# A decoder layer with 64 experts on one core: the expert rows found from a list of places, the second tile of an expert woven into the next expert's step

## The reference

```python
router_logits = x2d @ gate_w                      # 800 rows, 64 experts
routing_weights = jax.nn.softmax(router_logits, axis=-1)
routing_weights, selected_experts = jax.lax.top_k(routing_weights, TOP_K)   # 8 of 64
routing_weights = routing_weights / jnp.sum(routing_weights, axis=-1, keepdims=True)
...
layer_w0 = jax.lax.ragged_dot(sorted_inputs, gate_k, group_sizes, preferred_element_type=jnp.bfloat16)
layer_w1 = jax.lax.ragged_dot(sorted_inputs, up_k, group_sizes, preferred_element_type=jnp.bfloat16)
intermediate = jax.nn.silu(layer_w0) * layer_w1
expert_out = jax.lax.ragged_dot(intermediate, down_k, group_sizes, preferred_element_type=jnp.bfloat16)
...
out = jnp.einsum('tke,tk->te', unsorted, routing_weights.astype(jnp.float32))
```

## Time and profile before

| | |
|---|---|
| time, median of 3 runs | 2540.93 us (2531.51 to 2547.09) |
| span of the profiled execution | 2527.7 us |
| what lies around the span, against the median | 13.2 us |
| mean granted clock of TensorE | 0.897 of full speed |
| PE busy | 2011.5 us (80%) |
| DVE, ACT, POOL busy | 45%, 26%, 19% |
| DMA | 518.81 MB, mean 205 GB/s |

### The profile page before, as it was taken

One profiled execution on the slowest core, in us unless ns is written; L12 is line 12 of the kernel. 1 busy time (PEld: TensorE's weight loads), 2 busy tenths in 40 slices (PEclk: granted clock), 3 DMA queues, 4 the chain that ended last, 5 costly groups with the idle time before them and its releaser, 6 DMA issues. The chain is left out here.

```text
span 2527.7 us, 48690 instructions
## 1 busy us (share of the span) xinstructions
PE 2011.5 (80%) x17744; PEld 1692.7 (67%) x17745; DVE 1130.7 (45%) x2122; ACT 646.6 (26%) x1391; POOL 468.2 (19%) x556
## 2 busy tenths in 40 slices
PE   5999886059298989999959899959857788877756
PEld 4999864037298978888758777736656666666622
DVE  4444510034233354444433566643365555554366
ACT  4333300033221234434321344431101111111112
POOL 0111101101000011111100111101133334332156
PEclk9999988569699989999979999979979999999965
DMA  7999997669987255555276587833459989898445
GB/s 183 214 215 222 218 239 253 235 187 228 268 215 159 78 121 137 121 129 129 66 190 162 150 198 184 191 108 81 163 181 366 353 314 416 335 373 343 176 147 161
DMA packets 148152, 518.81 MB, mean 205 GB/s; under 512 B 27154, under 2 KB 68114, under 8 KB 140858
## 3 DMA queue, kind: packets, MB, share of 16 engines
q0 software_dynamic: 31776, 215.85, 38.2%
q1 hardware_dynamic: 105162, 281.04, 30.7%
q10 hardware_dynamic: 11088, 20.19, 2.1%
HBM read 582.94 MB, written 236.06 MB: 324 GB/s over the span
## 5 line engine op out<-in xcount | busy, mean ns | idle before, releaser
L81 PE MATMUL img_acc<-img_ctx_hi,img_w_hi 128*128 128x258 f32 x1024 | 303.4, 296 | 51.4 <-DVE img_ctx_lo L1158 40.1
L82 PE MATMUL img_acc<-img_ctx_lo,img_w_hi 128*128 128x258 f32 x1024 | 295.0, 288 | 0.1
L83 PE MATMUL img_acc<-img_ctx_hi,img_w_lo 128*128 128x258 f32 x1024 | 294.7, 288 | 0.0
L1780 POOL DMA_DIRECT2D experts_bf_dram<-in_moe_dram x192 | 98.3, 512 | 871.7 <-DMA experts_bf_dram<-in_moe_dram 542.2
L81 PEld LDWEIGHTS img_acc<-img_ctx_hi,img_w_hi 128*128 128x128 f32 x1024 | 199.8, 195 | 76.1 <-issue 65.4
L1951 POOL DMA_INDIRECT moe_rows<-expert_rows_dram,moe_index x77 | 150.3, 1952 | 387.1 <-DVE moe_index L2101 382.6
L82 PEld LDWEIGHTS img_acc<-img_ctx_lo,img_w_hi 128*128 128x128 f32 x1024 | 199.9, 195 | 0.4 <-issue 0.4
L83 PEld LDWEIGHTS img_acc<-img_ctx_hi,img_w_lo 128*128 128x128 f32 x1024 | 200.0, 195 | 0.0
L81 PE MATMUL txt_acc<-txt_ctx_hi,txt_w_hi 128*128 128x320 f32 x512 | 169.5, 331 | 37.5 <-DVE txt_ctx_lo L1158 29.2
L82 PE MATMUL txt_acc<-txt_ctx_lo,txt_w_hi 128*128 128x320 f32 x512 | 161.8, 316 | 0.0
L83 PE MATMUL txt_acc<-txt_ctx_hi,txt_w_lo 128*128 128x320 f32 x512 | 161.7, 316 | 0.0
(11 more groups left out here) (321 smaller groups left out, 4332.9 us busy)
## 6 DMA issues: line engine op xcount, KB each, us to landing
experts_bf_dram<-in_moe_dram POOLq DMA_DIRECT2D x192, 768.0 KB, 8.5
routing_w<-experts_bf_dram SPq DMA_DIRECT2D x48, 2304.0 KB
moe_w_last<-experts_bf_dram SPq DMA_DIRECT2D x16, 2304.0 KB
expert_results_dram<-self_zeros POOLq DMA_DIRECT2D x19, 1536.0 KB
self_w_raw<-in_w_self_dram SPq DMA_DIRECT2D x32, 512.0 KB, 12.0
expert_results_dram<-moe_out ACTq DMA_DIRECT2D x64, 256.0 KB, 7.3
img_raw<-in_ctx_img_dram SPq DMA_DIRECT2D x8, 1032.0 KB, 6.3
cross_k_dram<-img_kT SPq DMA_DIRECT2D x64, 129.0 KB, 2.0
```

The lines of the kernel that those rows point to most:

```text
L81: eng.matmul(out, w_hi, a_hi, start=first, stop=False)
L82: eng.matmul(out, w_hi, a_lo, start=False, stop=False)
L83: return eng.matmul(out, w_lo, a_hi, start=False, stop=last)
L1780: pool.dma_start(self.dst_d[n], self.src_d[n]).then_inc(self.done[u], 16)
```

## The change

- **Results.** Each expert has a fixed area of 7 tiles (`PLACES`), so a row's place in the results is known as soon as its rank in the expert is. Nothing is blanked, and `first_tile` goes.
- **Routing.** Choice, rank and place are found batch by batch in `route_phase`. POOL writes each row's number to its place in a list in DRAM: 8 scatters of 100 numbers a batch, in turn into four lists (`scatter`), each behind the last one of its list. At the end SP loads the four lists, DVE takes the least of them (an empty place holds 800), PE turns it, and the row numbers of all experts stand in SBUF (`r.token`).
- **Experts.** The comparison and the 32 matmuls of a step go; DVE copies two columns of `r.token` (`note_token`) for expert e+2, and POOL gathers e+2 in step e, where it was e+3. PE's step now is gate of e, narrow of e-1, up of e; if e-1 has a second tile, its transposes, products and narrow stand between these, with a PSUM tile of their own for the transposes. SP waits for `expert_done`, which DVE signals at the end of the step. Code for both cases stands in each step. The routing weights are made at the start, from the 8 chosen logits.
- **Combine** takes its places from `r.places`.

```diff
-            blank = clear_d.rearrange("(c n p) d -> c p n d", p=P, c=CLEARS)
-            pool.wait_ge(cleared, 3)
-            for c in range(CLEARS):
-                wait(pool, blanked, 16 * c)
-                pool.dma_start(blank[c], zeros[:, :].unsqueeze(1).broadcast_to(blank[c].shape)
-                               ).then_inc(blanked, 16)
-            pool.wait_ge(blanked, 16 * CLEARS)
...
-                wait(sp, at_split, b - 1)
+                wait(sp, outp_ready, 2 * (b - 1))
...
+            sp.wait_ge(router_ready, B)
+            for n in range(LISTS):
+                sp.wait_ge(listed[n], 16 * B * TOP_K // LISTS)
+                sp.dma_start(list_rows[:, n], list_d[n].rearrange("(e t p) n -> e t (p n)", e=EXPERTS, p=P)
+                             ).then_inc(list_loaded, 16)
+            sp.wait_ge(list_loaded, 16 * LISTS)
...
+                pool.dma_start(list_d[n].rearrange("(p n) one -> p (n one)", p=P), empty[:, :]
+                               ).then_inc(list_cleared, 16)
+            pool.dma_start(xn_d[B * S:B * S + 1, :], no_row[:, :]).then_inc(list_cleared, 16)
...
+            def scatter(b):
+                pool.wait_ge(places_ready, b + 1)
+                for k in range(TOP_K):
+                    wait(pool, listed[k % LISTS], 16 * (b * TOP_K // LISTS + k // LISTS))
+                    pool.sem_inc(scatter_step, 1)
+                    pool.indirect_dma_start(
+                        out=list_d[k % LISTS][:, :],
+                        out_offset=bass.IndirectOffsetOnAxis(ap=r.places[:, b, k:k + 1], axis=0),
+                        in_=numbers[:, b:b + 1], in_offset=None).then_inc(listed[k % LISTS], 16)
...
+            pool.wait_ge(list_cleared, 16 * LISTS + 16)
+            for b in range(B):
+                send(b, b % 2)
+                if b + 2 < B:
+                    add_bias(b + 2, b % 2)
+                if b > 0:
+                    scatter(b - 1)
+            scatter(B - 1)
...
+            def choose(b, u):
+                dve.wait_ge(logits_ready, b + 1)
+                link(dve.max(r.top[:, b, :], logits[:, u, :]))
+                dve.max_index(which[:, :], r.top[:, b, :], logits[:, u, :])
+                link(dve.match_replace(rest[:, :], r.top[:, b, :], logits[:, u, :], SELECTED))
+                dve.tensor_tensor(chosen[:, u, :], rest[:, :], logits[:, u, :],
+                                  ALU.not_equal).then_inc(chosen_ready, 1)
+                shape = [S, TOP_K, EXPERTS]
+                link(dve.tensor_tensor(match[:, :, :], expert_no[:, :].unsqueeze(1).broadcast_to(shape),
+                                       which[:, :].unsqueeze(2).broadcast_to(shape), ALU.is_equal))
+            def find_places(b, u):
+                shape = [S, TOP_K, EXPERTS]
+                dve.wait_ge(ranked, b + 1)
+                link(dve.tensor_tensor(place[:, :], rank_ps[0:S, 0:EXPERTS], place_start[:, :], ALU.add))
+                link(dve.tensor_tensor(so_far[:, :], so_far[:, :], chosen[:, u, :], ALU.add))
+                link(dve.tensor_tensor(match[:, :, :], match[:, :, :],
+                                       place[:, :].unsqueeze(1).broadcast_to(shape), ALU.mult))
+                link(dve.tensor_reduce(place_of[:, :], match[:, :, :], AX.X, ALU.add))
+                dve.tensor_copy(r.places[:, b, :], place_of[:, :]).then_inc(places_ready, 1)
...
+            find_places(B - 2, 0)
+            choose(B - 1, 1)
+            find_places(B - 1, 1)
+            dve.sem_inc(chosen_ready, 1)
+            dve.wait_ge(ranked, B + 1)
+            tabulate()
+            dve.wait_ge(list_loaded, 16 * LISTS)
+            link(dve.tensor_tensor(least[:, :, :], list_rows[:, 0], list_rows[:, 1], ALU.min))
+            link(dve.tensor_tensor(least[:, :, :], least[:, :, :], list_rows[:, 2], ALU.min))
+            dve.tensor_tensor(list_f[:, :, :], least[:, :, :], list_rows[:, 3], ALU.min).then_inc(list_ready, 1)
+            dve.wait_ge(list_turned, 1)
+            dve.tensor_copy(r.token[:, :, :].rearrange("p t e -> p (t e)"),
+                            list_ps[:, 0:MAX_TILES_OF * EXPERTS])
...
+            def rank(b, u):
+                wait(pe, places_ready, b)
+                pe.wait_ge(chosen_ready, b + 1)
+                pe.matmul(rank_ps[0:S, 0:EXPERTS], ones[:, :], so_far[:, :], start=True, stop=False)
+                pe.matmul(rank_ps[0:S, 0:EXPERTS], before[:, :], chosen[:, u, :],
+                          start=False, stop=True).then_inc(ranked, 1)
...
+    LAG = 1
+    AHEAD = 2
...
-                    wait(sp, out_ready, e - W_SLOTS + 1)
+                    wait(sp, expert_done, e - W_SLOTS + 1)
...
+                gather(g, c + AHEAD)
...
+            def note_token(e, c):
                 if has_expert(e):
-                    wait(dve, numbered, e - 1)
-                    compare(seated[:, c % 2], e, 2 * P).then_inc(seated_ready, 1)
-            def note_rows(e, c):
-                if has_expert(e):
                     wait(dve, turned, e - W_SLOTS + 1)
-                    dve.wait_ge(numbered, e + 1)
-                    dve.tensor_copy(index[:, c % W_SLOTS, :], number_ps[:, 0:2]).then_inc(index_ready, 1)
+                    wait(dve, expert_done, e - W_SLOTS + 1)
+                    dve.tensor_copy(token[:, c % W_SLOTS, :],
+                                    r.token[:, 0:2, bass.ts(e, 1)].rearrange("p t e -> p (t e)")
+                                    ).then_inc(token_ready, 1)
...
+                    tiles = tiles_of(dve, e - 1)
+                    with dve.If(tiles > 1):
+                        x = tiles_before(dve, e - 1)
+                        x_turn_rows(x)
+                        copy_right()
+                        x_multiply(x)
+                        multiply(e, c)
+                        x_copy_right(x, x_copied)
+                        behind_second(dve, e - 1, tiles, x, tile)
+                        dve.sem_inc(expert_done, 1)
+                    with dve.Else():
+                        copy_right()
+                        multiply(e, c)
+                        dve.sem_inc(x_copied, 1)
+                        dve.sem_inc(expert_done, 1)
+                else:
+                    multiply(e, c)
...
+                turn_rows(g, c + 1)
+                if has_expert(e - 1):
+                    tiles = tiles_of(pe, e - 1)
+                    with pe.If(tiles > 1):
+                        x = tiles_before(pe, e - 1)
+                        x_turn_rows()
+                        gate()
+                        narrow_first()
+                        x_products(x)
+                        up()
+                        pe.wait_ge(x_inner_ready, x + 1)
+                        pe.wait_ge(left_copied, e)
+                        pe.wait_ge(right_copied, e)
+                        narrow(slot, x_inner, x_out_ready)
+                        behind_second(pe, e - 1, tiles, x, tile)
                     with pe.Else():
-                        pe.sem_inc(x_numbered, 1)
-                    pe.wait_ge(x_landed, x + 1)
-                    pe.wait_ge(rowsT_ready, min(e + 2, EXPERTS) if isinstance(e, int) else e + 2)
-                    for k in range(KT):
-                        mm = pe.transpose(turn[:, k, :], rows[:, c % W_SLOTS, 1, k::KT], ident[:, :])
-                    mm.then_inc(x_turned, 1)
-                    pe.wait_ge(x_rowsT_ready, x + 1)
-                    pe.wait_ge(inner_ready, e + 1)
-                    products(c % W_SLOTS, c % 2, x_rowsT, (x_gate_ready, x_up_ready))
-                    pe.wait_ge(x_inner_ready, x + 1)
-                    wait(pe, left_copied, e)
-                    wait(pe, right_copied, e)
-                    narrow(c % W_SLOTS, x_inner, x_out_ready)
-                    pe.wait_ge(x_copied, 2 * x + 2)
-                    pe.sem_inc(x_done, 1)
-                further(pe, e, tile)
-            pe.wait_ge(chosen_ready, 1)
-            picks = chosen_bf[:, :, :].rearrange("s b e -> s (b e)")
-            pe.matmul(rank_ps[0:S, :], before[:, :], picks, start=True, stop=True)
-            pe.matmul(count_ps[:, :], ones[:, :], picks, start=True, stop=True).then_inc(ranked, 1)
-            for e in range(W_SLOTS):
-                pick_rows(e, e)
-            await_table(pe)
+                        gate()
+                        narrow_first()
+                        up()
+                else:
+                    gate()
+                    up()
```

More of the change, by code:

```diff
@@ L1595, in _ @@
                         load_x1(u, u)
-            with sp.Fori(1, B // 2) as g:
-                for u in range(2):
-                    load_at(2 * g + u, u)
-                    load_x1(2 * g + u, u)
+            for b in range(2, B):
+                load_at(b, b % 2)
+                load_x1(b, b % 2)
             for u in range(2):
@@ new lines, in _ @@
+            for e in range(AHEAD):
+                note_token(e, e)
+            shape = [S, B, TOP_K]
```

(35 more changed lines are left out.)

547 lines of the change are left out of this document (230 added, 317 removed).

## The result

The changed kernel takes 2687.9 us (median of 4 runs, 2678.5 to 2688.7), the kernel before 2539.7 us (4 runs): a ratio of 1.059, 95% interval 1.055 to 1.062. It is slower by 5.9%, where 2491 us and a range of 2400 to 2575 had been forecast. The span of the profiled execution is 2687.2 us, 159.5 more than before.

What follows compares the result with a forecast made beforehand. Blanking was taken to bound 420 to 510.7 us, and PE the experts' single-tile steps, with chained waits for second tiles. The span, 2527.7 - 87 + 20 + 17 = 2477.7, plus 13.2 around it gave 2491 us, range 2400 to 2575.

Steps and rivals of the forecast that it cites:

- Blanking: End of self-attention: without blanking the query stage starts at 423 instead of 510.7, -87 us.
- Routing: Routing to expert 1's transposes: scatters and list work with nothing beside them at the end, +20 us.
- The gather's cycle: Experts: each step lasts from transposes to the next gather's issue plus its landing, 8.1 us.
- the pairs: Experts with a second tile, 13 of them: the pair of gathers lands some 3 us later.
- Second tiles: Experts: a second tile's waits lie under other experts' matmuls, its step 9.6 us instead of 19.
- Clock and code: Experts: PE's lower clock and fetching of its longer code, +10 us; fetching 41 us at most.
- (C): Rival: gathers meet queued transfers throughout the experts, 10.0 us a step, 2584 us in all; chance 0.14.
- (B): Rival: the DMA engines bound the experts, not the gather's cycle; experts 480 us, 2386 us in all; chance 0.14.
- (D): Rival: blanking only hid another wait, the query stage starts no earlier than 495; 2563 us; chance 0.03.

Runs made afterwards that it cites:

- e4: The kernel before without its 19 blanking transfers and nothing else of the change: 2447.5 us, ratio 0.964.
- e6: e1 with TensorE's code for a third tile taken out: 2500.5 us, ratio 0.984.
- e5: The changed kernel without TensorE's code for a third tile, both arms of the branch kept: 2530.9 us, ratio 0.994.
- e7: e6 with the gathers issued one step earlier, of e+3 instead of e+2: 2366.1 us, ratio 0.930.
- e11: e7 with PE's loop twice, with and without a third tile's code, chosen by one branch ahead of it: 2369.1 us, ratio 0.937.
- e8: The kernel before with 32 never-executed matmul instructions more in each step: 2546.5 us, ratio 1.002.
- e10: e8 with 80 never-executed TensorE instructions added ahead of the loop: 2813.0 us, ratio 1.111.
- e1: The changed kernel with TensorE's code of a step written once instead of in each arm of one branch: 2626.8 us, ratio 1.036.
- e9: e1 with 160 never-executed TensorE instructions added ahead of the loop: 2516.3 us, ratio 0.994.
- e3: The kernel before with 160 never-executed matmul instructions more in each step: 2879.4 us, ratio 1.135.

## Why the prediction was wrong

By its own steps:

- **Blanking.** Forecast -87, bounds -91 to -80; the trace has -84.0, e4 alone -83. Right. The last stores of x1, issued from 412.70 on in 11.33 us, landed some 4 us later than I put them.
- **Routing.** Forecast +20, bounds +10 to +35; +26.6 in the changed kernel's trace, +17.7 in e6's. The scatters at the end came 1.28 us apart (1.3 forecast), the last at 1775.63 (1769). Three batches of them ran behind the last logits (1744.0), as worked out, but only two behind the last send (1755.40), where I had put all three. Right in size.
- **The gather's cycle.** Forecast: a step is 2.36 us to the gather's issue plus its landing, 8.1 us, 8.9 with the pairs. In e6, where code is resident, 52 steps take 499 us, 9.6 each. By the events of the gathers' semaphores the 39 of them that wait for a single gather hold 2.5 us to the issue, 6.1 to the landing and 0.8 behind it. The mechanism is right, and its term was too small: the stage takes +38 us in e6 (1789.70 to 2395.75) against +17, of which 10 were meant for clock and code. Two errors partly cancel in this. The 30 steps that neither wait for a pair nor hold a second tile take 9.1 us, 1.0 more than forecast, and a second tile adds some 2.3 us to its two steps, where I had put 4.5. The issue took 0.95 to 1.0 us in nearly all of the gathers, as expected without DVE's comparison.
- **Second tiles.** No window of 13 us for one is left: in e6 the 13 steps that wait for a pair of gathers take 10.1 us each, and the 13 that hold a second tile's work 10.8. Right.
- **Clock and code, +10 us.** This step failed. I had seen that the pass of 2064 was longer than the 1510 that stay resident, but priced fetching by the image stage, where 9 blocks in 89.5 us cost 2.9 us of PE's time, and called 41 us its upper bound. That loop (1675 instructions, 8 blocks) is itself fetched again on every pass, but it has no branch inside: PE needs a new block only every 13 to 14 us, and the fetch keeps ahead. Here a single step jumps over some 380 instructions, its target isn't there, and PE stands for some 5 us, in most steps on the path. The trace of the changed kernel has 187 us of idle time by "issue". By the medians the fetching costs 157 us (e5) where I had added 10 and allowed 41; the 188 us between the spans of the changed kernel and e6 hold another 30 for the two arms. The bound came from a row of another kind of code; such a price should have stood in a rival with its own weight. I had put it into (C) in half a sentence, at 0.14 with the rest.
- **Rivals.** (C), 2584 us, names the right side, but mostly another cause: queues on full DMA engines, where the trace has them busy for 0.65 only and the loss goes with the fetching of code. (B), 2386 us, is near what e7 and e11 came to (2366 and 2369) once the gathers were issued a step earlier. (D) is refuted by e4.
- **The sum.** With e6's terms: -84.2 + 17.7 + 38.0 and -0.5 for combine give -28.9 with rounding, its span (2498.8 against 2527.7). Without the fetching the changed kernel takes 2531 us (e5), 40 from the forecast and inside the range; with its code written once as well it takes 2500 (e6), 9 from it. With the fetching, the range was missed by 113 us.
- **Luck in the 9 us.** The forecast span was 2477.7, and e6's is 21 us longer. Of the 13.2 us that I added for what lies around the span, e6 shows 1.5 (2500.3 for the profiled execution against its span of 2498.8); the rest was only that the profiled execution of the kernel before was faster than its median. This error hides more than half of the difference.

## What to carry to other kernels

A loop's code is a resource like a buffer: count the instructions of a pass in the compiled program, those in branches that never run among them, and keep the pass below what stays resident (1498 and 1512 did here; 1626 and 1629 did or didn't, by where they began). If the rule of the table holds, a pass of up to 1537 instructions touches at most 7 blocks wherever it begins (an estimate: six blocks and one instruction). Write what both arms of a branch do once, outside of it (e6 against e5, 30 us), and put rare cases into a second copy of the loop (e11). Idle time by "issue" with packets of the instruction queue in the same stretch means code; look for that pair before anything else when no engine and no queue is full.

When a producer is moved nearer to its consumer, compare the whole way from issue to landing with the step: one step more of lead was worth 134 us here.

## What the runs showed of the hardware that I had not expected

- Eighty instructions that are never executed, ahead of a loop, made it slower by 267 us (e8 against e10), and 160 made another faster by 110 us (e1 against e9): only the loop's place in the 16 KB blocks differs.
- A loop that overflows loses nearly all of its blocks, not the one too many: e1, which touches 8, fetched 9 packets in every four steps, and e9, which touches 7, none between the twelfth step and the loop's end.
- The same overflow costs little where no jump stands inside the pass: the image stage's loop is fetched again on every pass too, 9 packets in 89.5 us, and PE is busy for 86.6 of them.
- PE stands at the start of a missing block even in the midst of a group of matmuls: in e3 for 2.8 to 6.5 us, 36 times at four places.
- PE's granted clock follows its busy share: 0.76 in the changed kernel's experts (busy for 59%), 0.84 in e6 (68%), 0.93 in e7 (81%).
